# Output projection for two tiles in one pass from split halves, and rope's turned product in one VectorE operation

## What is computed

```python
for i in range(6):
    x = attn_layer(shift_tokens(x), Wqkv[i], q_scale[i], k_scale[i], Wo[i]) + x
    x = ffn_layer(shift_tokens(x), ln_g[i], ln_b[i], W1[i], b1[i], W2[i], b2[i]) + x

def attn_layer(x, Wqkv, qs, ksc, Wo):      # 16 heads of 64, windows of 32 tokens
    q, k, v = split(x @ Wqkv)              # 128 -> 3 * 1024
    q, k = l2norm(q) * qs, l2norm(k) * ksc
    q = q * cos * scale + rotate_half(q) * sin * scale      # rotate_half: (x1, x2) -> (-x2, x1)
    k = k * cos / scale + rotate_half(k) * sin / scale
    return local_attention(q, k, v) @ Wo   # each window sees itself and the window before; 1024 -> 128
```

## Time and profile before

| | |
|---|---|
| median of 3 runs | 3935.38 us (3933.94 to 3938.61) |
| the profiled execution | 3928.65 us, its span 3926.6 us |
| busy PE, DVE, POOL, ACT | 3690.6, 3058.0, 2597.4, 2270.7 us |
| share of the span | 94%, 78%, 66%, 58% |
| mean granted TensorE clock | 0.986 of full |

### The profile page before, as it was taken

How to read it: one execution, slowest core, us unless ns; L and a number is a source line. 1 busy time by engine, 2 the same in 40 slices (tenths; PEclk the granted TensorE clock), 3 DMA queues, 4 the chain that set the end, 5 groups by cost and what they waited for, 6 DMA issues and landing times.

```text
span 3926.6 us, 163773 instructions
## 1 busy us (share of the span) xinstructions
PE 3690.6 (94%) x67712; PEld 2844.7 (72%) x67712; DVE 3058.0 (78%) x5829; ACT 2270.7 (58%) x4270; POOL 2597.4 (66%) x3029
## 2 busy tenths in 40 slices
PE   5999979999999999999999999999999999999998
PEld 3555557777767777677877678787677876777876
DVE  7666658888778888788887788887788887888876
ACT  3555546666546666456666366665466664566653
POOL 4545538787547887367887288775477873687870
PEclk8999989999999999999999999999999999999999
DMA  1000002222212222122222122222122221222220
GB/s 44 4 6 4 6 28 68 56 60 60 58 32 59 59 57 59 41 49 60 61 57 56 30 65 57 59 61 58 32 60 58 59 56 41 54 57 58 60 52 22
DMA packets 136313, 189.08 MB, mean 48 GB/s; under 512 B 38006, under 2 KB 58484, under 8 KB 135412
## 3 DMA queue, kind: packets, MB, share of 16 engines
q1 hardware_dynamic: 135540, 178.23, 17.7%
HBM read 22.67 MB, written 2.10 MB: 6 GB/s over the span
## 4 chain that ended last, share of the span: by engine, by line
PE 76%; issue 4%; DVE 2%; POOL 2%; ACT 0%; DMA 0%; POOLq 0%; SPq 0%; DVEq 0%; ACTq 0%
PE PS L1270 18%; PE PS L1417 10%; PE PS L1256 10%; PE PS L1294 8%; PE PS L1280 8%; PE PS L1258 8%; PE PS L1257 8%; PE PS L1476 2%; PE PS L1411 2%; PE PS L1454 1%; PE PS L1447 1%; POOL t L1182 1%; PE PS L1442 1%; POOL t L1187 0%; DVE m L1800 0%
## 5 line engine op out<-in xcount | busy, mean ns | idle before, releaser
L1182 POOL TENSOR_TENSOR t<-t 128x1024 f32<-128x1024 f32 x384 | 908.0, 2370 | 363.9 <-DVE t L1762 362.6
L1187 POOL TENSOR_TENSOR t<-t,rn 128x1024 f32<-128x1024 f32 x384 | 723.6, 1905 | 29.8 <-POOL rn L150 27.3
L1542 ACT ACTIVATE va<-PS 128x512 f32<-128x512 f32 x384 | 229.8, 599 | 614.4 <-PE PS L1258 611.6
L1760 DVE TENSOR_TENSOR t<-PS,rope 128x512 f32<-128x512 f32 x768 | 523.2, 681 | 26.1 <-ACT sq L1577 24.5
L1256 PE MATMUL PS<-w_hi,xh 128*128 128x512 f32 x1152 | 514.2, 446 | 22.3 <-DVE xl L1063 11.3
L1577 ACT ACTIVATE sq<-PS 128x512 f32<-128x512 f32 x768 | 454.1, 593 | 33.0 <-PE PS L1258 17.7
L1270 PE MATMUL PS<-constants,t 128*128 128x128 f32 x3072 | 443.8, 277 | 19.8 <-POOL t L1187 12.8
L1258 PE MATMUL PS<-w_lo,xh 128*128 128x512 f32 x1152 | 458.5, 398 | 0.0
L1257 PE MATMUL PS<-w_hi,xl 128*128 128x512 f32 x1152 | 457.5, 397 | 0.0
L1767 DVE TENSOR_REDUCE ss<-sq 128x16 f32<-128x1024 f32 x384 | 448.3, 1209 | 0.0
L1270 PEld LDWEIGHTS PS<-constants,t 128*128 128x128 f32 x3072 | 351.9, 141 | 68.9 <-POOL t L1187 15.9
(11 more groups left out here) (168 smaller groups left out, 7869.8 us busy)
## 6 DMA issues: line engine op xcount, KB each, us to landing
vs<-va SPq DMA_DIRECT2D x768, 130.0 KB
vs<-va SPq DMA_DIRECT2D x768, 65.0 KB
t<-in_L_ffn_Wqkv SPq DMA_DIRECT2D x18, 512.0 KB, 4.4
w_out<-in_L_ffn_Wo SPq DMA_DIRECT2D x6, 512.0 KB, 3.9
a_normed<-in_L_attn_x SPq DMA_DIRECT2D x8, 256.0 KB, 7.0
a_xo<-in_L_attn_x SPq DMA_DIRECT2D x8, 256.0 KB, 2.8
out<-total SPq DMA_DIRECT2D x8, 256.0 KB, 3.5
w_raw<-in_L_ffn_W SPq DMA_DIRECT2D x6, 341.0 KB
```

The lines of the kernel that those rows point to most:

```text
L1182: pool.tensor_tensor(mine[:, i, :], mine[:, i, :], t2[:, i, :], ALU.add).then_inc(done, 1)
L1187: pool.tensor_tensor(h, h, bc(rn[:, H * i:H * (i + 1)], 2, HB), ALU.mult).then_inc(done, 1)
L1760: dve.tensor_tensor(o1, src, bc(rope[:, 2 * i, t, :], 1, 8), ALU.mult)
```

## The change

1. **Output projection.** The weights are split like the others into `wo_hi` and `wo_lo`. The mixed, turned values of two tiles are kept side by side: ACT copies the float32r high part `oh`, and DVE subtracts it from PSUM for the low part `ol` (new, two operations of 512 columns per tile, between the last rope half and `lengths`). In slots with odd t only, PE makes 24 float32r matmuls of 256 columns for both tiles, after both score halves. DVE adds 256 columns to the state, in odd slots only.
2. **Rope.** The turned product is one operation of 512 columns without the exchange. POOL makes the exchange: its one addition of 1024 columns becomes two of 512 in strided halves. The sine table changes sign, and the six scale loads per layer become two.
3. **Around it.** `Wo` is loaded into the first half of `sq` and split between layers by ACT (`high_out`) and POOL (`low_out`); the first values of a layer wait for that. `on` lives in `pw`, so the exponentials wait for `ot_mm` in place of `pt_mm`. K projections also wait for `ol_made`.

```diff
-        w_out = sb("w_out", [P, PAIRS, D])
+        wo_hi, wo_lo = sb("wo_hi", [P, PAIRS, D], F32R), sb("wo_lo", [P, PAIRS, D], F32R)
+        wo_raw = sq[:, 0, :].rearrange("p (j d) -> p j d", j=PAIRS)
-        on = sb("on", [P, PAIRS, 2, HB])
-        oT = sb("oT", [P, PAIRS, P])
+        on = pw
+        oh, ol = sb("oh", [P, PAIRS, 2 * P], F32R), sb("ol", [P, PAIRS, 2 * P], F32R)
...
 # POOL, rope_and_scale
                 def add(i, roped, done):
                     pool.wait_ge(roped, at(T, 0, 2, 2))
-                    pool.tensor_tensor(mine[:, i, :], mine[:, i, :], t2[:, i, :], ALU.add).then_inc(done, 1)
+                    sum_of, other = (v[:, i, :].rearrange("p (h a d) -> p h a d", h=H, a=2) for v in (mine, t2))
+                    pool.tensor_tensor(sum_of[:, :, 0, :], sum_of[:, :, 0, :], other[:, :, 1, :], ALU.add)
+                    pool.tensor_tensor(sum_of[:, :, 1, :], sum_of[:, :, 1, :], other[:, :, 0, :], ALU.add).then_inc(done, 1)
...
+            def low_out(lay):
+                pool.wait_ge(wo_hi_made, lay + 1)
+                pool.tensor_tensor(wo_lo[:], wo_raw, wo_hi[:].bitcast(F32), ALU.subtract).then_inc(wo_lo_made, 1)
...
+            low_out(0)
             scale_rope(0)
...
 # PE, slot
-                pe.wait_ge(attn_done, at(T, 3, 1, 1))
+                if t % 2 == 0:
+                    pe.wait_ge(attn_done, at(T, 3, 1, 1))
+                pe.wait_ge(ol_made, at(T, 3, 2, 2))
...
                     score_half(0)
-                if mix:
-                    pe.wait_ge(oT_made, at(T, 2, 2, 2))
+                    score_half(1).then_inc(s_mm, 1)
+                if mix and t % 2:
+                    pe.wait_ge(ol_made, at(T, 2, 2, 2))
                     for pair in range(PAIRS):
-                        last = pe.matmul(PS[:, y_at, 0:P], w_out[:, pair, :], oT[:, pair, :],
-                                         start=(pair == 0), stop=(pair == PAIRS - 1))
-                    last.then_inc(y_mm, 1)
-                if score:
-                    score_half(1).then_inc(s_mm, 1)
+                        for w, o in ((wo_hi, oh), (wo_hi, ol), (wo_lo, oh)):
+                            last = pe.matmul(PS[:, y_at, 0:2 * P], w[:, pair, :], o[:, pair, :],
+                                             start=(pair == 0 and o is oh and w is wo_hi),
+                                             stop=(pair == PAIRS - 1 and w is wo_lo))
+                    last.then_inc(y_mm, 2)
...
 # DVE
                 dve.tensor_tensor(o1, src, bc(rope[:, 2 * i, t, :], 1, 8), ALU.mult)
-                dve.tensor_tensor(o2[:, :, 0:32], src[:, :, 32:64], bc(rope[:, 2 * i + 1, t, 0:32], 1, 8), ALU.mult)
-                dve.tensor_tensor(o2[:, :, 32:64], src[:, :, 0:32], bc(rope[:, 2 * i + 1, t, 32:64], 1, 8),
-                                  ALU.mult).then_inc(done, 1)
+                dve.tensor_tensor(o2, src, bc(rope[:, 2 * i + 1, t, :], 1, 8), ALU.mult).then_inc(done, 1)
...
+                if 2 in ages:
+                    for c in range(2):
+                        dve.wait_ge(oh_made, at(T, 2, 2, c + 1))
+                        if t % 2 == 0:
+                            dve.wait_ge(y_mm, at(T, 3, 1, 1))
+                        now = slice(4 * c, 4 * (c + 1)), slice(P * (t % 2), P * (t % 2 + 1))
+                        dve.tensor_tensor(ol[:, now[0], now[1]],
+                                          PS[:, (0 if ending else 4) + c, :].rearrange("p (j q) -> p j q", j=4),
+                                          oh[:, now[0], now[1]].bitcast(F32), ALU.subtract).then_inc(ol_made, 1)
+                if 0 in ages:
                     lengths(T)
...
-                if 2 in ages:
+                if 2 in ages and t % 2:
                     dve.wait_ge(y_mm, at(T, 2, 1, 1))
...
-                    dve.tensor_tensor(now, PS[:, 2 if ending else 4, 0:P].unsqueeze(1), now, ALU.add).then_inc(attn_done, 1)
+                    dve.tensor_tensor(now, PS[:, 2 if ending else 4, 0:2 * P].unsqueeze(1), now, ALU.add).then_inc(attn_done, 2)
```

More of the change, by code:

```diff
@@ L77, in constants @@
     for s in (q, k):
-        tables += [np.concatenate([cos * s, cos * s], 1), np.concatenate([-sin * s, sin * s], 1)]
+        tables += [np.concatenate([cos * s, cos * s], 1), np.concatenate([sin * s, -sin * s], 1)]
     rope = np.stack(tables).astype(np.float32).reshape(4, TPS, P, HB).transpose(2, 0, 1, 3)
@@ L964, in windowed_layers @@
         hi1_made, lo1_made = sem("hi1_made"), sem("lo1_made")
+        wo_hi_made, wo_lo_made = sem("wo_hi_made"), sem("wo_lo_made")
         xh_made, xl_made = sem("xh_made"), sem("xl_made")
@@ L986, in windowed_layers @@
         ot_mm = sem("ot_mm")
-        oT_made = sem("oT_made")
+        oh_made, ol_made = sem("oh_made"), sem("ol_made")
         y_mm = sem("y_mm")
@@ L1165, in scale_rope @@
             def scale_rope(lay):
-                pool.wait_ge(scale_in, 96 * lay + 96)
+                pool.wait_ge(scale_in, 32 * lay + 32)
                 pool.wait_ge(rk_made, 2 * (lay * (B * TPS) + CREDIT))
@@ L1239, in step @@
                         split_rest(pool, lay + 1, 0, 0)
+                        pool.wait_ge(xl_made, 2 * halves(lay + 1, 0, 0) + 2)
+                        low_out(lay + 1)
                     if follows and old == 3:
@@ L1520, in layer @@
             def layer(lay, follows):
-                pe.wait_ge(wout_in, 16 * lay + 16)
+                pe.wait_ge(wo_lo_made, lay + 1)
                 attention(pe, lay, slot)
@@ L1572, in high_part, with high_out @@
                 copy(w_hi[:, third(i)], w_raw[:, third(i)]).then_inc(hi_made, 1)
+            def high_out(lay):
+                act.wait_ge(wout_in, 16 * lay + 16)
+                act.wait_ge(y_mm, lay * (B * TPS) + CREDIT)
+                copy(wo_hi[:], wo_raw).then_inc(wo_hi_made, 1)
             def square(T, i, c, bank, projected, done):
@@ L1589, in opening @@
                 i, c, bank = OPENING[n]
+                if n == 0:
+                    act.wait_ge(wo_lo_made, lay + 1)
                 if i == 2:
@@ L1599, in weigh @@
                 def weigh(c):
-                    act.wait_ge(pt_mm, at(T, 3, 2, c + 1))
+                    act.wait_ge(ot_mm, at(T, 3, 2, c + 1))
                     act.wait_ge(e_made, at(T, 2, 2, c + 1))
@@ L1651, in slot @@
                 if 2 in ages:
-                    act.wait_ge(y_mm, at(T, 3, 1, 1))
+                    if p == 0:
+                        act.wait_ge(y_mm, at(T, 3, 1, 1))
                     if ending:
@@ L1656, in slot @@
                         act.wait_ge(ot_mm, at(T, 2, 2, c + 1))
-                        pairs(oT, c, (0 if ending else 4) + c, oT_made)
+                        pairs(oh[:, :, P * p:P * (p + 1)], c, (0 if ending else 4) + c, oh_made)
                     if ending:
@@ L1696, in step @@
                             high_part(lay + 1, THIRDS[2 * old + a])
+                        if follows and 2 * old + a == 3:
+                            high_out(lay + 1)
                 feed_forward(act, step)
@@ L1708, in _ @@
             act.wait_ge(made, 6)
-            copy(credit[:, 47:48], zeros[:, 0, 0:1]).then_inc(gel_made, 2)
+            copy(credit[:, 47:48], zeros[:]).then_inc(gel_made, 2)
             act.preload_act_table_set("natural_log_exp_and_others")
@@ L1714, in _ @@
                 high_part(0, i)
+            high_out(0)
             for n in range(len(OPENING)):
@@ L1839, in slot @@
                         hidden(lay, 0, 0, j)
-                if 2 in ages:
+                if 2 in ages and t % 2:
                     dve.wait_ge(y_mm, at(T, 2, 1, 1))
                     dve.wait_ge(ffn_done, lay * B + s2 + 1)
-                    now = state[:, bass.ds(s2, 1), 1 + P * tile2:1 + P * (tile2 + 1)]
-                    dve.tensor_tensor(now, PS[:, 2 if ending else 4, 0:P].unsqueeze(1), now, ALU.add).then_inc(attn_done, 1)
+                    now = state[:, bass.ds(s2, 1), 1 + P * (tile2 - 1):1 + P * (tile2 + 1)]
+                    dve.tensor_tensor(now, PS[:, 2 if ending else 4, 0:2 * P].unsqueeze(1), now, ALU.add).then_inc(attn_done, 2)
                 if ending:
```

15 lines of the change are left out of this document (6 added, 9 removed).

## The result

| | before | changed |
|---|---|---|
| median of 4 runs | 3935.26 us (3933.94 to 3938.61) | 4181.27 us (4173.68 to 4188.75) |
| profiled execution, span | 3926.6 us | 4181.8 us |
| mean granted clock | 0.986 | 0.971 |

The changed kernel is slower: ratio 1.0624 [1.0603, 1.0645], +246 us. The direction was as forecast, the size was not: +95 us had been forecast, and 4110 us was the upper end of the range.

A forecast was written before the change was run, and what follows sets the result against it. The loop through PE's scores and DVE's maximum, not PE's 94%, was taken as the bound. Loop 100, start 4, stalls -20, clock 14 gave +98, rounded to +95: 4024 us on the profiled execution, forecast 4030, range 3965 to 4110.

The forecast's parts named there:

- The ring: Loop from PE's scores over DVE's maximum to PE's next scores: a pair of slots 28.78 us against 27.74, +100 us.
- Rope gives nothing: DVE's rope operations: 0.06 us less per half, 0.24 per slot, but hidden by waits, so no gain.
- POOL's half: One of POOL's two additions of 512 columns: 1.28 us, so +0.2 us per former addition, covered by later sums.
- step 1: Odd slot, maximum to maximum: 13.87 us with the old projection taken out, new one and state addition put in, 15.11 us.
- step 2: Small stalls of 0.67 us per slot: a third of them in 96 odd slots hidden by PE's new idle time, -20 us.
- step 3: Lower clock behind PE's new idle time in odd slots: one in ten of 96 loses 1.5 us, +14 us.
- Faster: PE is the bound, and its work falls 1.08 us per pair: 3832 us, or some 3890; chance 0.11.
- By the weight load: Projection matmuls cost 0.189 us each, +1.7 us per pair, +160: about 4190 us; chance 0.07 together with POOL's strided halves.
- Slower still by the clock: Half of the odd slots drop to the lower clock and lose 1.7 us each: +82, about 4100 us; chance 0.10.
- POOL's rival: At 1.9 us per strided half POOL bounds what PE turns: +77, about 4100 us; chance 0.07 together with the weight load.
- the alternation: Sign of being right: DVE's maximum alternates between about 14.3 and 15.8 us from start to start, a pair at 30.
- signs of being wrong: Equal slots under 14.5 us; L1429 over 3.5 us; PE idle before turns ended by POOL; attention clock below 0.95.

The follow-up runs named there:

- split_before_seed: The changed kernel with ACT's split of the next half ahead of the seed that waits for `half_ss`: 4143.5 us, ratio 1.0555.
- y_behind_scores_alone: The kernel before with only its old float32 output projection moved behind both score halves, still in every slot: 4065.67 us, ratio 1.0347.
- y_between_halves: The changed kernel with the 24 projection matmuls of odd slots put between the two score halves: 4081.45 us, ratio 1.0387.
- projection_alone: The changed kernel with the old rope, so only the output projection's part of the change: 4184.31 us, ratio 1.0649.

## Why the prediction was right in direction and wrong in size

**Right.** The ring. PE's 94% was not the bound, and PE's work fell while the time rose. The even slot's shortest step is 13.46 us where 13.67 was worked out, with the maximum right behind `half_ss`. The new matmuls cost 0.117 us each where 0.12 was taken; the weight load did not add to them. Rope gives nothing (1.001 [0.9994, 1.0027]). POOL's half costs 1.28 us and is covered. `low_out(0)` at the start was to cost 4 us and cost 1 in the two profiled executions (the first maximum at 601.0 in place of 599.9 us); over all traces the first maximum comes at 597.1 to 599.9 us without it and at 599.4 to 605.1 with it, so 4 is possible too.

**Wrong, step 1: "From 13.87 I take the old projection (1.98) ...: 15.11 us".** The shortest odd step is 15.60. The 0.49 us that lack are ACT's. The sum took the way from the maximum to the weights over from the kernel before, 2.89 us; in odd slots it is now 3.30 (median), and 2.81 once ACT's order is mended. I followed the late sums to POOL and the scaled q, found them covered, and did not ask who else waits for `half_ss`. ACT does, in its queue, with the split, a copy and a square ahead of the exponential. The prediction had put the wait down to DVE's subtraction by the earlier trace rows, which are the weight loads' waits; the row of PE itself in the new timeline names ACT's exponential. split_before_seed took 0.5 us off the odd step (0.34 where the clock stayed up, and only 0.18, to 15.42, off the shortest, so that 15.60 - 15.11 is the same 0.49 is partly luck). The price is some 30 to 45 us: 27 by that run, 0.43 to 0.49 x 96 by the steps.

**Wrong, step 2: "Of the 0.67 us per slot some happen while PE would now idle anyway ... -20 us".** The term has the wrong sign. I took the stops as given and asked only which would be hidden. They depend on the order: two halves of 64 score matmuls with the projection between have 6 stops over 0.4 us in the program, 128 in a row have 61. PE's idle time before the score matmuls put down to issue went from 8.2 to 96.8 us, and all PE idle put down to issue from 0.77 to 1.98 us per pair. They come after PE's idle time of the slot, on the ring, so nothing hides them. What PE waits for there is its next 256 instructions: the old projection's 1.98 us between the halves had covered that transfer, and the prediction counted these 1.98 us only as work. y_behind_scores_alone shows it on the kernel before and y_between_halves on the changed one. Their price is some 60 to 90 us: 93 - 35 = 58 for the odd slots alone by y_between_halves, 137 - 48 = 89 by y_behind_scores_alone, each with the lower clock that followed the stops.

**Wrong, step 3: "If one in ten of 96 loses 1.5 us: +14 us".** That the lower clock would come behind idle time of PE was right; behind which, and how often, was not. 29 of 84 odd slots had a stretch at the lower clock. 27 such stretches begin in them. Four begin behind the idle time before the weights, the one that the prediction named; 20 begin within 1.7 us behind a stop in the scores of 1.5 to 2.1 us, and three behind another stop by issue. So most of it is a consequence of step 2. The earlier trace rows were thin ground for the price, too: PE had idled 11.3 us only shortly before them, and the clock had been at 0.50 until 578 us. Odd slots without a stretch at the lower clock took 17.16 us on average, all of them 17.71; 0.55 x 96 = 53 us. That is a comparison of slots and not an experiment. Of the two idle times of the disturbed slot, it was the second, in the scores, behind which the clock was lower; the stretch behind the first was at 1.00:

```profile
1971.60:1973.00 1.40, 1.39 (x9) 1.22 (x10) 1.40 (x3) 1.40 (x4) 1.28 (x1) 1.00 0.00 0
```

The Trainium skill, TensorE: Matmul & The Clock Gate, section "Why this matters for your kernels", warns of idle gaps between bursts; the first gap here, 1.81 us long, brought no lower clock and the second, 1.84 us, did.

Together: 100 (ring) + 1 + about 40 (ACT) + about 75 (stops) + about 35 for what of the clock is not in the 75 already = 251 us, against 246 measured. The last three are rough, since they overlap, and the 35 is not measured: behind the first 600 us the trace has 134 us more at the lower clock than before, which bounds its price at half of that, 67 us. The ring's 100 is borne out: the shortest steps of a pair went from 27.54 to 29.06 us, and without ACT's 0.49 that is 1.03 x 96 = 99 us (129 if only the 0.18 is taken off that split_before_seed gave at the shortest step). Of the prediction's terms the ring was right, ACT's was absent, that of the stops had the wrong sign, and that of the clock was less than half.

**The rivals.** Faster is out: DVE's slack was indeed too small. "By the weight load" named 4190 us, the right size for a wrong reason, since the matmuls cost 0.117 us each; that is luck. "Slower still by the clock" named 4100 and is partly true. POOL's rival falls with projection_alone.

Of what was to show it, the alternation, the 1 us wait of the addition in quiet slots, L1429 at 2.9 us per pair in quiet slots and PE below 94% came true. The odd step did not (17.7, not 15.8), DVE's share did not rise above 78% (77%, of a longer span), and the idle time before the odd slots' weights was ended by ACT, not DVE. None of the signs of being wrong came, not even a granted clock below 0.95: the lowest mean of a layer's attention was 0.97. That last row was the sign of step 1.

## What to carry to other kernels

When a wait moves an engine's result later, list every reader of that result, and for each the work queued behind its wait; one reader that is covered says nothing about the next. Treat stalls that the profile calls issue as depending on the order of the instructions. Count the engine's instructions from one stop to the next: if the distances are multiples of 256, it is waiting for its next instructions, and before taking a long matmul out from between two runs of small ones, ask whether the merged run still lasts as long as that transfer. Work that is moved behind the critical scores, even if it is shorter, puts everything that can go wrong in it on the ring.

## What was not expected of the hardware

- A run of 128 small matmuls (64x64, each with its own weight load, 1.91 us for all of them at 1823.91) stops in the middle for up to 2.1 us in about a third of the slots, never ahead of the 70th. A run of 64 with longer matmuls before it hardly ever does. The stops lie at multiples of 256 records and end 1.15 to 1.75 us after a packet of 16,384 bytes of instructions has landed. The Trainium skill, Runtime: NRT & Kernel Launch, section "Instruction fetch mechanics", says that instructions are fetched in blocks of 256 and that this is hidden by the pace of issue. The traces agree on the 256 and contradict the "hidden" for dense runs of small matmuls. No run moved the multiples of 256 by adding instructions to PE's program, and what fills the 1.4 us (median) between the landing and PE's going on stays open.
- Idle times of nearly the same length, 1.81 and 1.84 us in one slot, were followed by a granted clock of 1.00 and of 0.50. No run shows what decides between them.
- One rope operation of 512 columns in place of two of 256 took 0.60 us in place of 0.66 from start to start, but POOL's addition in two halves of 1.28 us costs more than its one of 2.35.
